# First layer of a four-layer graph network: count steps set between halves of turns and look-ups, look-ups two groups ahead, a ring of five messages

## The reference, cut to what matters

```
r1 = x[src] * edge_attr ;  out  = segment_sum(r1, dst)
r2 = x[dst] * edge_attr ;  out += segment_sum(r2, src)
x  = layernorm(x + out)
```

## Time and profile before

| | |
|---|---|
| median of three runs | 2361.65 us (2359.45 to 2366.54) |
| profiled execution | 2367.35 us, span in the trace 2365.5 us |
| first layer's loop (first gather of the loop to last put) | 121.63 to 1113.5 us |
| engines' busy share of the span | PE 66%, DVE 59%, POOL 57%, ACT 30% |
| GpSimd's DMAs in the loop | 440 puts (L800), 264 gathers (L786) |

### The profile page before, as it was taken

One profiled execution on the slowest core, in us unless ns is written; L12 is line 12 of the kernel. 1 busy time (PEld: TensorE's weight loads), 2 busy tenths in 40 slices (PEclk: granted clock), 3 DMA queues, 4 the chain that ended last, 5 costly groups with the idle time before them and its releaser, 6 DMA issues.

```text
span 2365.5 us, 41588 instructions
## 1 busy us (share of the span) xinstructions
PE 1559.0 (66%) x7812; PEld 1070.9 (45%) x7813; DVE 1398.2 (59%) x4868; ACT 718.0 (30%) x1290; POOL 1350.1 (57%) x1329
## 2 busy tenths in 40 slices
PE   3135777777777677766787733666555465699995
PEld 3034444444444444443676622555544455355453
DVE  8736766766666766677676655544454554624325
ACT  0001554555555555555000011222221222232231
POOL 0067776777777777777777527777777773000000
PEclk9978665665665665676899865655565657799997
DMA  1333444444444444444798612222222221442320
GB/s 44 70 91 91 127 119 115 128 123 118 127 122 123 122 119 123 121 138 122 214 249 229 164 42 54 54 53 52 53 53 50 52 52 25 167 165 105 138 106 27
DMA packets 332478, 251.07 MB, mean 106 GB/s; under 512 B 105297, under 2 KB 306621, under 8 KB 328699
## 3 DMA queue, kind: packets, MB, share of 16 engines
q1 hardware_dynamic: 224603, 118.11, 18.0%
q0 software_dynamic: 42240, 86.08, 13.5%
q10 hardware_dynamic: 65440, 45.04, 6.0%
HBM read 172.45 MB, written 78.22 MB: 106 GB/s over the span
## 4 chain that ended last, share of the span: by engine, by line
PE 35%; POOL 23%; issue 15%; DVE 10%; ACT 4%; ACTq 2%; DMA 2%; DVEq 2%; SPq 0%; POOLq 0%
POOL shared L826 19%; PE PS L1006 11%; PE PS L903 8%; PE PS L876 6%; PE PS L888 4%; POOL G L814 4%; ACT PS L1167 3%; PE PS L867 2%; DVE shared L1636 2%; DVE shared L1575 2%; ACT shared L1173 1%; ACTq L1180 1%; DVE stats L1683 1%; DMA shared<-record 1%; DVE X L1709 1%
## 5 line engine op out<-in xcount | busy, mean ns | idle before, releaser
L800 POOL DMA_INDIRECT record<-shared,IX x440 | 459.7, 1045 | 182.9 <-issue 153.5
L826 POOL DMA_INDIRECT shared<-table,src_of x440 | 442.1, 1005 | 189.4 <-issue 133.8
L903 PE MATMUL PS<-shared 128*128 128x400 bf16 x816 | 305.0, 471 | 175.6 <-ACT PS L1167 146.1
L786 POOL DMA_INDIRECT G<-in_x_dram,MET x264 | 269.1, 1019 | 200.0 <-DMA MET<-meta_d 119.8
L1167 ACT ACTIVATE PS<-PS,kept 128x400 f32<-128x400 f32 x407 | 230.9, 567 | 221.3 <-PE PS L903 206.2
L1173 ACT ACTIVATE shared<-PS 128x400 uint16<-128x400 f32 x408 | 205.8, 504 | 125.0 <-issue 124.4
L1636 DVE TENSOR_SCALAR shared<-iota_h,shared 128x400 bf16<-128x400 f16 x816 | 236.2, 330 | 0.0
L1086 PE MATMUL PS<-shared,G 128*128 128x128 f32 x880 | 214.2, 391 | 18.2 <-issue 6.9
L876 PEld LDWEIGHTS PS<-X,OHT 128*128 128x128 f32 x880 | 183.0, 308 | 64.6 <-issue 64.6
L876 PE MATMUL PS<-X,OHT 128*128 x880 | 209.4, 413 | 2.5 <-ACT OHT L1152 1.3
L814 POOL DMA_INDIRECT G<-in_x_dram,src_of x176 | 178.0, 1011 | 55.1 <-issue 50.3
(11 more groups left out here) (331 smaller groups left out, 2356.0 us busy)
## 6 DMA issues: line engine op xcount, KB each, us to landing
nearby<-shared ACTq DMA_DIRECT2D x408, 100.0 KB
shared<-in_edge_attr_dram SPq DMA_DIRECT2D x616, 64.0 KB
shared<-nearby SPq DMA_DIRECT2D x28, 1400.0 KB, 8.7
shared<-record SPq DMA_DIRECT2D x110, 258.0 KB, 3.5
MET<-meta_d SPq DMA_DIRECT2D x440, 2.0 KB
record<-shared,IX POOLq DMA_INDIRECT x440
shared<-table,src_of POOLq DMA_INDIRECT x440
G<-in_x_dram,MET POOLq DMA_INDIRECT x264
```

The lines of the kernel that those rows point to most:

```text
L786: pool.indirect_dma_start(G[:, d, j, 0:D], None, x[:, :], row_index(MET[:, q, j, SRC - D:SRC - D + 1].bitcast(U32))).then_inc(a.gather[d], 16)
L800: pool.indirect_dma_start(record2[:, :], row_index(IX[:, q, j:j + 1]), M[:, g, j, :], None, bounds_check=SLOTS - 1, oob_is_err=False).then ...
L826: pool.indirect_dma_start(G2[:, half, GROUP * q + j, :], None, table1[:, :], row_index(src_of[:, GROUP * n + j:GROUP * n + j + 1])).then_i ...
L903: t = pe.matmul(PS[:, bank_, 0:HI], LOW[:, g, h, :], VIN[:, g, h, :], start=False, stop=h == 1, skip_group_check=True)
```

## The change

- PE cuts its four transposes and its four look-up matmuls of a group into halves, and runs them between the steps: half of the turn, step 0, the rest of the turn, step 1, half of the look-up, step 2, the rest, step 3, and then the sum. The turn now runs three groups ahead (was two), the look-up two (was one).
- ACT's copy of the turned one-hots runs three groups ahead and moves from the front of the iteration to between the step pairs.
- DVE's places and one-hots run four groups ahead (were three). The part of `places` that computes the puts' addresses becomes a stage of its own, one group ahead, with waits on the puts of the half turn before the last.
- The messages M get a ring of five instead of two, with five semaphores; they are still made one group ahead. M1 becomes a tensor of its own.

```
-        M = ring(SIDES, ROW2)
-        M1 = ring(SIDES, D)
+        M = ring(DEEP, ROW2)
+        M1 = sb("M1", [P, SIDES, GROUP, D])
...
-        a = Sems("a", "onehot turned onehot_t looked_up scaled summed added", load=DEEP, gather=DEEP, put=SIDES)
+        a = Sems("a", "onehot turned onehot_t looked_up scaled summed added", load=DEEP, gather=DEEP, put=DEEP)
...
                 def load_records2(i, q):
                     if isinstance(i, int) and i == 0 and q == 0:
-                        for g in range(SIDES):
-                            sp.wait_ge(a.put[g], 16 * TILES // SIDES)
+                        for g in range(DEEP):
+                            sp.wait_ge(a.put[g], 16 * TILES // DEEP)
...
             def put_messages(i, q):
-                g = q % SIDES
+                g = q % DEEP
...
                 freed(pe, a.onehot_t, i, q, SIDES)
-                for j in range(GROUP):
+                for j in range(GROUP // 2):
+                    pe.transpose(PS[:, g, j * P:(j + 1) * P], OH[:, q % DEEP, j, :], ident[:, :])
+
+            def turn_a_rest(i, q):
+                g = q % SIDES
+                for j in range(GROUP // 2, GROUP):
                     t = pe.transpose(PS[:, g, j * P:(j + 1) * P], OH[:, q % DEEP, j, :], ident[:, :])
                 t.then_inc(a.turned, 1)
 
+            look_regs = []
+
             def look_up(i, q):
                 g, n = q % SIDES, group(i, q)
-                regs = columns(PE, columns_of[0], n)
+                look_regs[:] = columns(PE, columns_of[0], n)
                 pe.wait_ge(a.onehot_t, n + 1)
                 freed(pe, s_m2, i, q, SIDES)
-                for j in range(GROUP):
+                for j in range(GROUP // 2):
+                    pe.matmul(PS[:, 2 + g, j * P:(j + 1) * P], OHT[:, g, j * P:(j + 1) * P],
+                              X[:, bass.ds(look_regs[j], D)], start=True, stop=True)
+
+            def look_up_rest(i, q):
+                g = q % SIDES
+                for j in range(GROUP // 2, GROUP):
                     t = pe.matmul(PS[:, 2 + g, j * P:(j + 1) * P], OHT[:, g, j * P:(j + 1) * P],
-                                  X[:, bass.ds(regs[j], D)], start=True, stop=True)
+                                  X[:, bass.ds(look_regs[j], D)], start=True, stop=True)
                 t.then_inc(a.looked, 1)
...
-            pipeline(pe, (turn_a, 2), (step_pe(0), 0), (look_up, 1), (step_pe(1), 0), (sum_a, 0), (step_pe(2), 0), (step_pe(3), 0),
+            pipeline(pe, (turn_a, 3), (step_pe(0), 0), (turn_a_rest, 3), (step_pe(1), 0), (look_up, 2), (step_pe(2), 0),
+                     (look_up_rest, 2), (step_pe(3), 0), (sum_a, 0),
                      (prepare_pe, 0))
...
-            pipeline(act, (copy_turned, 2), (step_act(0), 0), (step_act(1), 0), (step_act(2), 0), (step_act(3), 0), (last_store, 0))
+            pipeline(act, (step_act(0), 0), (step_act(1), 0), (copy_turned, 3), (step_act(2), 0), (step_act(3), 0), (last_store, 0))
...
                 dve.tensor_copy(dloc[:, bass.ds(GROUP * n, GROUP * MANY)], flat(DL[:, at, :]))
+
+            def put_places(i, q):
+
+                if q % MANY:
+                    return
+                at, turn = slice(q, q + MANY), 2 * i + q // MANY
+                dve.wait_ge(s_dl, turn + 1)
+                if again(i):
+                    for d in range(DEEP):
+                        dve.wait_ge(a.put[d], 16 * GROUP * (turn - 1))
                 dve.tensor_scalar(inside[:, :, :], DL[:, at, :], 0.0, None, ALU.is_ge).then_inc(s_in, 1)
...
             def source_messages(i, q):
                 g, d, n = q % SIDES, q % DEEP, group(i, q)
-                if used(i, q, SIDES):
-                    dve.wait_ge(a.put[g], 16 * GROUP * use(i, q, SIDES))
-                dve.tensor_copy(M[:, g, :, D:ROW2].bitcast(I32), MET[:, q, :, SRC_IN_BLOCK - D:SRC_IN_BLOCK - D + 1])
+                if used(i, q, DEEP):
+                    dve.wait_ge(a.put[d], 16 * GROUP * use(i, q, DEEP))
+                dve.tensor_copy(M[:, d, :, D:ROW2].bitcast(I32), MET[:, q, :, SRC_IN_BLOCK - D:SRC_IN_BLOCK - D + 1])
...
-            pipeline(dve, (places, 3), (onehots_a, 3), (step_dve(0), 0), (source_messages, 1), (step_dve(1), 0), (target_rows, 0), (step_dve(2), 0),
+            pipeline(dve, (places, 4), (onehots_a, 4), (step_dve(0), 0), (put_places, 1), (source_messages, 1), (step_dve(1), 0), (target_rows, 0), (step_dve(2), 0),
                      (target_messages, 0), (step_dve(3), 0), (prepare, 0))
```

More of the change, by code:

```diff
@@ L1559, in source_messages @@
                 g, d, n = q % SIDES, q % DEEP, group(i, q)
-                if used(i, q, SIDES):
-                    dve.wait_ge(a.put[g], 16 * GROUP * use(i, q, SIDES))
-                dve.tensor_copy(M[:, g, :, D:ROW2].bitcast(I32), MET[:, q, :, SRC_IN_BLOCK - D:SRC_IN_BLOCK - D + 1])
+                if used(i, q, DEEP):
+                    dve.wait_ge(a.put[d], 16 * GROUP * use(i, q, DEEP))
+                dve.tensor_copy(M[:, d, :, D:ROW2].bitcast(I32), MET[:, q, :, SRC_IN_BLOCK - D:SRC_IN_BLOCK - D + 1])
                 dve.wait_ge(a.load[d], 16 * GROUP * (use(i, q, DEEP) + 1))
                 dve.wait_ge(a.looked, n + 1)
-                dve.tensor_tensor(M[:, g, :, 0:D], PS[:, 2 + g, :].rearrange("p (j f) -> p j f", f=D),
+                dve.tensor_tensor(M[:, d, :, 0:D], PS[:, 2 + g, :].rearrange("p (j f) -> p j f", f=D),
                                   R[:, d, :, 0:D], ALU.mult).then_inc(s_m2, 1)
```

## The result

The changed kernel takes 2318.02 us (median of four runs, 2317.42 to 2324.12), the kernel before beside it 2363.09 us (four runs, 2359.45 to 2366.54): a ratio of 0.983, 95% interval 0.981 to 0.985, or 45 us less. The forecast was 2325 us in a range of 2308 to 2352. The profiled execution took 2324.12 us with a span of 2322.3; before it was 2367.35 with 2365.5, so between the two traces lie 43 us.

What follows compares the result with a forecast made beforehand. The prediction took a PE, ACT and DVE chain as the loop's pace, with 42 us of GpSimd stalls: 42 less 4 (chain's excess after lead) less 1.3 (start) is 37, so 2361.65 - 37 = 2325 us, range 2308 to 2352.

Steps and rivals of the forecast that it cites:

- What bounds the kernel before: First layer's loop: a chain of PE, ACT and DVE sets the pace at 90.4 us a turn; GpSimd follows.
- GpSimd's pace: GpSimd in the first layer's loop: 1.333 us for one DMA with its gap, 85.3 us for a turn's 64.
- the bound of shorter first puts: Lower bound: first puts behind a stall, 1.30 to 1.56 us long, shrink to the 1.04 mean; 29 x 0.26 = 8 us.
- The full group: Loop's chain: 8.6 to 9.2 us a full group against 9.7; open sum and additions add 1.2 to 1.8.
- The excess of 9 us, less 5 from the lead: Loop: chain 1.0 us a turn over GpSimd for 8.74 turns; message lead pays 5 us, 4 stay lost.
- The start: Loop's start: put 2's message stands behind the wait for integers, so it begins at 155.6, 1.3 us later.
- The integers of a half turn: DVE's places, twice a turn: integers needed a group earlier; nothing in the steady loop, 4.2 us each if uncovered.
- rival 5: Slower: integers come late, 4.2 us twice a turn, turn of 94.7, 2401 us with the start; chance 0.10.
- The end: Behind the last put: next stage's 176 gathers have no slack, so it starts and ends earlier by the puts' gain.
- rival 3: GpSimd alone is the bound: no stall and shorter first puts, 2310 to 2313 us; chance 0.09.
- Rival 2: TensorE's slow prices only: full groups of 9.2 us, a turn of 88.5, 2344 us (to 2352); chance 0.20.
- Rival 4: No change: sum behind step 3 costs the look-up's gain, full group stays 9.7 us, 2355 to 2368; chance 0.08.

## Why the prediction was right, point by point

**What bounds the kernel before** held: a chain at 90.4 us a turn, with GpSimd behind it; with half of the gathers the turn stays at 90.6. (Of the 29 stalls one, 1.15 us at 412.08, stands ahead of another put than a group's first.)

**GpSimd's pace**, 1.333 us for a DMA and 85.3 a turn, came out at 1.344 and 85.9. The puts did not shrink from 1.045 us, and the gathers went from 1.019 to 1.030, so the bound of shorter first puts (8 us) was not to be had. Lengthening cost some 4 us: 440 x 0.003 + 264 x 0.011.

**The full group** was mis-sized. The chain's turn was forecast at 84.1 to 88.5, taken as 86.3, and is 80.0. Of the 4.1 us to the lower bound, 6 x (8.6 - 8.04) = 3.4 are the full groups, 4 x (7.4 - 7.23) = 0.7 the late ones and 0.2 the jump, within rounding. The term that was sized wrong is what a full group has beyond a late one. Its line behind step 3, 3.9 us, is near its forecast of 4.0 to 4.6; but a late group's line takes 3.1 where 2.8 was counted, so the sum and the additions add 0.8 and not 1.2 to 1.8. The forecast mixed slow and fast prices of TensorE as they stood before, while the clock rose with the change. Whether the clock explains the difference no run shows. So "almost equal" was wrong: the chain has 6 us a turn to spare.

**The excess of 9 us, less 5 from the lead**, thus did not exist: all 42 us of stalls went, not 38, and the ring had nothing to cover in the loop. Where VectorE waited for a gather's rows in the kernel after, it began some 1.7 us behind the end of the gather's last instruction, where the forecast counted 3 for a landing.

**The start** was right in place and small in size: put 2 begins at 156.5, 2.2 us later and not 1.3. VectorE had the integers at 153.78 instead of 153.36, and its message ends at 154.94 + 0.68 = 155.62, where 155.5 was counted. What was left out is what follows: the put begins 0.92 us behind the message, not 0.13. A put that waited stands 0.9 to 1.1 us behind its message elsewhere too (611.21 + 0.69 to 612.86 above). The forecast's own rows had this delay: in the kernel before, put 2 waited for the same integers as VectorE, which used them at 153.36, and it began at 154.33, 0.97 later. (The row names VectorE's L1544, but that makes the addresses of groups 5 to 9; those of put 2 were there from the start.) With 0.97 in place of 0.13 the sum would have said 156.5.

**The integers of a half turn** were on time (nothing idle ahead of L1548), so rival 5 is refuted. But their price of 4.2 us was read off the wrong load: the one issued at 149.13 is group 10's. The one that VectorE waited for until 153.36 is group 9's, behind the lanes:

```profile
143.91 1.95 SPq L663 DMA_DIRECT2D MET<-meta_d  x4
```

That is 9.4 us from issue to use. Without the lanes ahead it is 3.7 (136.85 to 140.54 above), so 4.2 came out about right by luck, and "the queue's first filling" was the lanes. ScalarE's copy and VectorE's places cost nothing that reaches GpSimd.

**The end** held: GpSimd goes from the last put to the next stage with 0.31 us between, and that stage ends earlier by all that the puts gained.

The sum by the two traces: 42 of stalls, less 2.2 at the start and some 4 to 5 for longer DMAs, is 35 at the last put (1112.5 to 1077.3). The next stage's gathers gave 5.3 more (231.9 us before, 226.6 after), with 1.011 us each before and 0.989 after. The change does not touch this stage: with the ring alone it took 228.9 us, and 229.0 without the ring, so I take this for scatter between executions, though no run shows its cause. The last 2.6 lie behind it. The direction was that of the forecast, a chain that no longer makes GpSimd wait; its 37 us stand against 35 in the loop and 43 to 45 in all.

**The rivals.** The result lies between the forecast and rival 3, GpSimd alone (2310 to 2313). In mechanism it is rival 3, to which 0.09 was given: no stall at all, with GpSimd the bound from group 3 on, though without that rival's shorter first puts. Rival 2, the slow prices, needed a falling clock and got a rising one. Rival 4, the lost cover of the additions eating the gain, is refuted: a full group takes 8.04 us and not 9.7, and putting the sum back behind step 1 costs 2.9 a turn. That the forecast came within 7 us is in part luck: the chain was sized 6.3 us a turn too long, which cost the sum only the 4 us of excess because GpSimd's pace hides the rest, and the 8 us behind the loop were in no term.

## What to carry to other kernels

Where an engine waits at each group for another, find its own pace first (instructions by duration and gap) and then the chain's, by an experiment that takes work from the engine and nothing from the chain: here the full kernel could show only 86 us, while the chain behind it had gone from 90.6 to 80.0. Give a result that crosses engines one more group of lead before rearranging the pieces of work around it; the same rearrangement cost 12 us a turn without the lead and 1.6 with it (one execution each). And once an engine without slack is the bound, look at what it waits for at the start: one large load behind the small ones it needed, instead of ahead of them, gave 10 us for a changed digit.

## What the runs showed of the hardware that was not expected

TensorE's granted clock rose although its batches were cut: from 0.61 to 0.79 between 240 and 360 us (0.74 there in a second execution of the changed kernel). The windows from 400 to 500 us with half of the gathers, first before, then with only the halves and the sum moved:

```profile
400.00:500.00 100.00, 69.98 (x264) 42.83 (x262) 66.98 (x242) 49.99 (x96) 57.53 (x55) 0.60 0.38 106
```

```profile
400.00:500.00 100.00, 62.24 (x239) 40.56 (x239) 61.25 (x219) 45.83 (x88) 51.29 (x51) 0.62 0.36 101
```

and with the new leads, first whole pieces, then the change:

```profile
400.00:500.00 100.00, 66.61 (x322) 42.52 (x322) 79.70 (x289) 59.60 (x117) 71.70 (x68) 0.81 0.48 132
```

```profile
400.00:500.00 100.00, 63.87 (x317) 43.03 (x315) 76.99 (x280) 58.83 (x116) 69.44 (x65) 0.83 0.46 127
```

Halves and the moved sum make 0.02 of difference in either pair; the new leads, with the ring and the copy's place, make 0.2. PE's busy share is about the same in all four (62 to 70 of 100 us), but where its clock is high it does 20 to 35% more matmuls in it (317 and 322 against 264 and 239). The Trainium skill (Perfetto Trace Analysis, "Matmul Optimizations") says that matmuls should run back to back in batches since the engine's power follows its use. Batches of four ran at 0.60 and at 0.81 here, so their size is not what the change of clock followed. Whether cutting them costs some of it these runs leave open. The pair that differs in the pieces alone, with the sum early in both, reads from 300 to 900 us, first whole, then in halves:

```profile
300.00:900.00 600.00, 399.95 (x1908) 256.87 (x1907) 472.63 (x1704) 354.49 (x692) 431.82 (x400) 0.80 0.47 131
```

```profile
300.00:900.00 600.00, 394.77 (x1797) 282.09 (x1798) 444.53 (x1606) 336.99 (x653) 400.39 (x378) 0.74 0.45 124
```

With all gathers and the later lanes it is the other way in the same window, 0.73 whole and 0.77 in halves (there the sum moves too). Whether the shorter waits raised the clock, or the higher clock shortened the waits, they do not separate, since the two came together in every variant.
